# Two changes of order in a DLRM tower kernel: ids ahead of tables in SP's queue, and one half of layer 2 behind the last grams

## What is computed

```python
e = jnp.stack([tbl_0[ids[:, 0]], ..., tbl_25[ids[:, 25]]], axis=1)       # 2048 x 26 x 128
combined = jnp.concatenate([dense_features[:, None, :], e], axis=1)      # 27 features of 128
interactions = jnp.einsum('bfd,bgd->bfg', combined, combined)
z = concat([dense_features, interactions[:, iu, ju]])                    # pairs f < g
h = concat([z, dense_features])
h = jnp.maximum(h @ W_top1 + b_top1, 0.0)                                # 607 -> 512
h = jnp.maximum(h @ W_top2 + b_top2, 0.0)                                # 512 -> 256
y = h @ W_top3                                                           # 256 -> 1
```

## Time and profile before

| | us |
|---|---|
| median of 3 runs | 359.95 |
| the profiled execution's own time | 359.83 |
| its span | 358.0 |
| PE busy | 325.9 (91%) |
| DVE busy | 240.7 (67%) |
| ACT busy | 183.7 (51%) |
| POOL busy | 250.0 (70%) |
| PE's share of the chain that ended last | 81% |

### The profile page before, as it was taken

One profiled execution on the slowest core, in us unless ns is written; L12 is line 12 of the kernel. 1 busy time (PEld: TensorE's weight loads), 2 busy tenths in 40 slices (PEclk: granted clock), 3 DMA queues, 4 the chain that ended last, 5 costly groups with the idle time before them and its releaser, 6 DMA issues.

```text
span 358.0 us, 10391 instructions
## 1 busy us (share of the span) xinstructions
PE 325.9 (91%) x4192; PEld 312.3 (87%) x4192; DVE 240.7 (67%) x721; ACT 183.7 (51%) x360; POOL 250.0 (70%) x264
## 2 busy tenths in 40 slices
PE   0558789999999999999999999999999999999576
PEld 0548679989999998999899999999899999998565
DVE  3889987996469762995389654986299556951012
ACT  1345555556633763457534664557445664366224
POOL 5777777777777777777777777777777777775020
PEclk9987999999999999999999999999999999999989
DMA  5999657664447434662457444653356344421230
GB/s 146 235 249 246 157 160 193 158 168 133 99 101 181 115 76 103 139 170 69 99 120 187 95 82 106 149 149 69 103 131 185 82 98 102 125 68 46 34 78 0
DMA packets 48069, 44.80 MB, mean 125 GB/s; under 512 B 26790, under 2 KB 42150, under 8 KB 48022
## 3 DMA queue, kind: packets, MB, share of 16 engines
q1 hardware_dynamic: 38448, 26.89, 31.8%
q0 software_dynamic: 8320, 16.87, 19.5%
q10 hardware_dynamic: 1254, 0.39, 0.6%
HBM read 39.33 MB, written 4.78 MB: 123 GB/s over the span
## 4 chain that ended last, share of the span: by engine, by line
PE 81%; DVE 7%; DMA 6%; SPq 2%; ACT 2%; issue 1%; POOL 0%; ACTq 0%
PE ps_o L335 39%; PE ps_m L386 16%; PE ps_g L375 15%; PE ps_t L346 7%; DVE onehot L749 5%; DMA oh_ids<-onehot_ids 3%; DVE tbl_lo L734 2%; DMA interaction_scratch<-inter 2%; PE ps_m L416 2%; SPq L207 1%; DMA x<-interaction_scratch 1%; PE ps_g L446 1%; POOL interaction_scratch L190 0%; SPq L228 0%; ACT emb L555 0%
## 5 line engine op out<-in xcount | busy, mean ns | idle before, releaser
L313 POOL DMA_INDIRECT rows<-tables,idx x256 | 247.4, 966 | 80.4 <-issue 76.9
L749 DVE TENSOR_SCALAR onehot<-oh_ids,rownum 125x256 fp32r<-125x256 int32 x640 | 200.2, 388 | 50.9 <-PE ps_o L335 43.1
L335 PE MATMUL ps_o<-onehot,tbl_hi 125*128 125x256 f32 x640 | 163.9, 295 | 22.0 <-DVE tbl_lo L734 21.8
L335 PE MATMUL ps_o<-onehot,tbl_lo 125*128 125x256 f32 x640 | 159.0, 287 | 0.0
L335 PEld LDWEIGHTS ps_o<-onehot,tbl_hi 125*128 125x128 f32 x640 | 125.0, 195 | 27.3 <-DVE tbl_lo L734 23.3
L335 PEld LDWEIGHTS ps_o<-onehot,tbl_lo 125*128 125x128 f32 x640 | 125.4, 196 | 0.0
L555 ACT ACTIVATE emb<-ps_o 128x256 f32<-128x256 f32 x80 | 49.3, 740 | 87.0 <-PE ps_o L335 87.0
L375 PEld LDWEIGHTS ps_g<-emb 128*54 128x54 f32 x2048 | 53.6, 130 | 4.8 <-issue 1.8
L375 PE MATMUL ps_g<-emb 128*54 128x54 f32 x2048 | 56.0, 214 | 1.8 <-ACT emb L581 0.8
L571 ACT ACTIVATE emb<-ps_t 128x512 f32<-128x512 f32 x63 | 45.8, 729 | 9.9 <-PE ps_t L346 9.6
L595 ACT ACTIVATE inter<-ps_g 128x432 f32<-128x432 f32 x64 | 33.9, 532 | 15.6 <-PE ps_g L375 13.1
(11 more groups left out here) (60 smaller groups left out, 206.5 us busy)
## 6 DMA issues: line engine op xcount, KB each, us to landing
oh_ids<-onehot_ids SPq DMA_DIRECT2D x80, 128.0 KB
rows<-tables,idx POOLq DMA_INDIRECT x256, 2.4
x<-interaction_scratch SPq DMA_DIRECT2D x23, 117.0 KB
inter<-small_tables SPq DMA_DIRECT2D x4, 448.0 KB
interaction_scratch<-inter SPq DMA_DIRECT2D x30, 47.2 KB
x<-small_tables SPq DMA_DIRECT2D x3, 448.0 KB
h<-small_tables SPq DMA_DIRECT2D x3, 448.0 KB
interaction_scratch<-inter SPq DMA_DIRECT2D x32, 38.2 KB
```

Of the source, the lines that this page charges most:

```text
L313: pool.indirect_dma_start(rows[e][:, k, :], None, tables[k], bass.IndirectOffsetOnAxis(ap=idx[:, NG * hh + k:NG * hh + k + 1], axis=0),).t ...
L335: mm = pe.matmul(o, tbl[p][:, k, c, :], onehot[n % SLOTS_OH][:, c, :], start=(c + p == 0), stop=(c == TCHUNKS - 1 and p == 1))
L749: op = nc.vector.tensor_scalar(onehot[n % SLOTS_OH][:, c, :], oh_ids[0:TPART, n % IDS, :], rownum[:, c:c + 1], None, ALU.is_equal)
```

## The change

Two edits, both only of order. In SP's queue, the ids of table 2 move ahead of table 1 (they were behind it), and the ids of table 3 move from behind tables 2 and 3 to between table 1 and the identity. In PE's last body, half 0 of layer 2 of block 6 moves from ahead of the last transposes to behind the last grams, next to half 1.

```diff
             load_ids(0)
             load_stage(sp, 0)
             load_ids(1)
+            load_ids(2)
             load_stage(sp, 1)
-            load_ids(2)
+            load_ids(3)
             sp.dma_start(ident[:, :], identity).then_inc(ident_loaded, 16)
             load_stage(sp, 2)
             load_stage(sp, 3)
-            load_ids(3)
             load_dense(0)
             load_ids(4)
             load_ids(5)
@@
                 transposes(b, 1)
                 grams(a)
                 transposes(b, 2)
-                layer2(m, 0)
                 last_transposes()
                 grams(b)
+                layer2(m, 0)
                 layer2(m, 1)
                 layer3(m)
```

## The result

The changed kernel takes **357.29 us** (median of 20 executions, 356.15 to 359.49); the kernel before, on the same chip, 359.69 us (20 executions, 358.60 to 361.28). The ratio is 0.9941, 95% interval 0.9929 to 0.9953: 2.1 us faster by the ratio, and the two medians lie 2.4 us apart, where 0.85 us was forecast. That is outside the range given. The profiled execution took 358.47 us (span 356.7), against 359.83 (span 358.0) before, so it shows 1.4 us of the gain. It is also 1.2 us slower than the median of its own kernel; what makes the others faster differs from one execution to the next, and most of the experiments are about that.

What follows compares the result with a forecast made beforehand. PE was taken to bound the kernel, with DVE's ids wait at the start and POOL's gathers close behind. Of 2.1 + 1.43 us freed, the last gather leaves 0.85: 359.1 us on the median, range 358.4 to 361.0.

Steps and rivals of the forecast that it cites:

- Edit 1, freed at the start: Start of the program: DVE gains about 2.1 us of its 2.73 us wait for ids 3, reaching PE in full.
- the landing of ids 4 at 20.98: SP's queue at the start: ids 4 land two small loads after 19.38, so DVE waits about 0.7 us.
- The prices of 3.03 us for a table and 0.80 for ids: SP's queue: landing times per load, 0.80 taken from three small loads and table 4 landing between 19.38 and 24.80.
- The sum: Last body: the gains do not add; 0.85 us gained at the grams of 3.5 us freed on PE.
- nothing in between: Between start and last body: edit 1's 2.1 us arrives whole, PE finishing group 2's transposes near 326.8, then waiting.
- The slack: End of the gather stream: last gather lands at 329.69, PE transposes its tile at 330.60, leaving 0.91 us.
- The last gather and the grams: Last body: L362 waits for the last gather, runs at about 330.05; grams begin near 330.85 instead of 331.69.
- the whole gather stream 0.3 us later: POOL: the moved split of table 3 holds a gather longer; bounds 0.1 us earlier to 1.0 later.
- everything behind the grams keeps its lengths: Tail behind the last grams: copies, stores, reload and last layers take as long as before.
- The clock before the last grams: Rival, 27%: PE's clock falls in the new idle time; last grams at half clock cost 2.0 to 3.4 us more.
- The slipped stream: Rival, 13%: POOL loses a whole hold, 1.1 instead of 0.3 us; 0.05 us of gain left, 359.9 us.
- The gathers bind less: Rival, 10%: holds shift in POOL's favour by up to 1 us, or only edit 2 works; 358.0 to 358.8 us.

Runs made afterwards that it cites:

- edit 1's trace: Only the SP queue reorder of ids, layer 2 left in its old place, against the kernel before: 359.20 us, ratio 0.9975.
- Edit 2 alone: Only layer 2's half 0 moved behind the last grams, ids in their old place, against the kernel before: 358.25 us, ratio 0.9968.
- the warmed one: Changed kernel plus 28 matmuls, result unread, between layer 2's halves and layer 3 of block 6: 356.94 us, ratio 0.9926 to the kernel before.
- padding: Small float32 matmuls behind block 0's first transposes: 36 in the kernel before, 366.52 us; 28 with both edits, 360.78; 8 instead, 359.13 and 356.78.

## Why the prediction was too small, step by step

**Edit 1, freed at the start: 2.1 us forecast, 2.8 measured.** The term that was mis-sized is the landing of ids 4 at 20.98. DVE began their one-hot at 19.48 without waiting. The prices of 3.03 us for a table and 0.80 for ids came from one span of landings, and that span was misread: SP issued table 4 only at 13.08 us, once the split of table 0 had freed its stage, so the landings from 19.38 to 24.80 are not one run of the queue. After the change it was issued at 12.10 and rounded by ACT at 22.11, not 24.80. Landings also differ between executions: in the six profiles with SP's queue in its old order the one-hot of table 4 begins between 21.39 and 23.05 us, in the nine others between 19.14 and 20.33. The 2.8 us are therefore those of this pair of profiles. It made no difference to the end, as the next step shows. The Trainium skill (SBUF — State Buffer, SBUF: two separate sides) would have had DVE wait for gathers, and the prediction worked out 1.2 us of gain from that. The trace speaks against it for that direction: the splits took 1.26 and 1.27 us, and 2.79 us were gained at block 0.

**The sum: "nothing in between" was wrong.** The slack was read at the last gather alone. In each body the transposes of the last group (L346) need their gathers too, and in edit 1's trace PE waits for one already at 48 us. PE did not arrive at L357 two us early and wait there; it waited in blocks 4, 5 and 6 (0.47, 0.60 and 0.47 us), layer 3 of blocks 3, 4 and 5 was 2.09, 1.27 and 0.57 us earlier than before, and PE came to L357 at 328.42 with no wait. The result at the grams is the same, since the last gather decides there.

**The last gather and the grams: right, 0.24 us off.** L362 was forecast at 330.05 and ran at 329.80, with the wait of 0.83 us foretold (0.8); the step to the grams was 0.81 us (0.80). The difference comes from the "0.3 us later" of the gather stream: in this profile it came 0.13 us earlier instead, and landed 0.11 us more slowly. The landing took 2.51 us; for it the Trainium skill (DMA: Bandwidth & Descriptors, Anatomy of one DMA — SWDGE (gpsimd) path) gives an estimate of 2.15 us, which is too short here.

**Edit 2 alone: right, but for 0.1 us.** 1.1 to 1.2 us forecast, 1.03 measured; 2.9 us of layer 2 behind the grams stayed hidden under ACT's issue (5.04 us, as in the earlier trace rows).

**The step that failed: the two terms that were held nearly fixed, "the whole gather stream 0.3 us later" and "everything behind the grams keeps its lengths".** In the profiled execution they explain all of the miss: the grams 0.24 us earlier than forecast, and the tail 0.29 us shorter, so that 1.08 + 0.29 are its 1.37 us.

*The gather stream.* Its bounds were 0.1 us earlier to 1.0 later. The last gather was issued at 327.16 and 326.84 in the two profiles of the changed kernel and at 326.50 in the warmed one, which is the same program up to there: 0.13, 0.45 and 0.79 us earlier than before. How many gathers a two-input DVE instruction holds differs from one execution to the next. In the kernel before, the slack of 0.91 us hides that; in the changed one PE waits for the last gather, so it goes into the time.

*The tail.* It varies between 23.6 and 25.2 us, with causes that no duration on the chain before shows: where the transfer of instructions falls, and how long the clock is down behind PE's wait for `relus2`. Both edits bring the start of the grams nearer and move 12 matmuls into that wait, which shortens it from 4.50 to 3.08 us.

*The rest of the median.* The median execution was 1.2 us shorter than the profiled one, and only one execution in each set has a trace. Still, the tail cannot be all of it. Behind the tail come 1.55 us more in every profile, so with the grams at 330.61 and the shortest tail of all fifteen profiles (23.63) the span would be 355.8 us. Eleven of the 20 executions have a shorter span, down to 354.3, which would put their grams at 329.1 with that same tail. So in these the gathers that PE waits for must have come earlier too, unless their tails were shorter than any seen. The clock goes with the times as well: of the 20, the 5 with a mean clock of 1.00 have a median of 356.31 us, the 11 at 0.995 (as profiled) 357.19, the 4 at 0.99 358.73. How the 1.2 us divide between stream and tail stays open.

**The rivals.** The clock before the last grams did not fall (1.00 from 331 to 335 us). The idle time had been spread over blocks 4 to 6, in pieces of about 0.5 us, instead of gathering at L357; that this is why the clock held isn't shown. The slipped stream did not come. "The gathers bind less", at 10% and with 358.0 to 358.8 us, had the part that came true, holds that shift in POOL's favour; it covers the profiled 358.47, but not the median.

**What stays open:** how the missing part of the median divides, and what decides whether the transfer of instructions goes out before or behind PE's wait. That a late transfer and a late reload go together in fifteen profiles, that four packets of band 2's stores then end just behind it, and that padding moves both is shown. That these four stand in line behind it on one DMA engine is the likely reading, but the traces kept here don't name the engine of a packet.

## What to carry to other kernels

Slack against a second stream is to be read at every place where the two meet, not at the last one alone: an advance won at the start is eaten piece by piece at such places (from 2.79 to 0.57 us here). Once a stream bounds the kernel, its own scatter goes into the time; read its last item from several profiles (325.59 to 327.29 us here) before giving it a range. A tail that is a chain of small stores and reloads has no fixed length; before pricing an edit ahead of it, line up the windows of clock and queues there, and ask what the edit does to the wait in it. Where PE idles just ahead of such a tail, a few unread matmuls in the gap can be worth about as much (0.27% in the kernel before) as either of these edits alone; here they moved the transfer of instructions as well as the clock.

## What the runs showed of the hardware

- Instructions come in transfers of 16 KB (33 here; by their count, PE's). When one fell among the small stores of a chain, four of the 128 store packets ended 0.5 to 0.9 us later than the last packet otherwise did, and the rounding behind the reload began at 16.5 to 16.8 instead of 15.4 to 16.1 us behind the grams.
- A gather that starts while a two-input DVE instruction runs is held almost to its end, by up to 1 us (1.96 instead of 0.94 us at 45.50 us in the kernel before). A split that meets a gather is at most 0.07 us longer (1.27 against 1.20 us).
- A small float32 matmul (128 x 128 by 128 x 32) costs 0.23 us at full clock (8 of them 1.87 us), as two records, so that 28 or 36 of them are no cheap padding.
- At the head, a fall of the clock cost nothing measurable (ratio 1.0002 with it taken away); in the tail the profiles with 6.8 us of it and an early transfer are 1.0 to 1.4 us longer than those with 3.4 us.
